# Second graph layer of a two-layer GNN and mixture-of-experts kernel: the scaling of the attention output moves from VectorE to ScalarE

## The reference, cut to what matters

```
x = x + L0_gnn(layernorm(x), adj)
x = x + L0_ffn(layernorm(x))            # 8 experts, top 2, 512 hidden
x = x + L1_gnn(layernorm(x), adj)       # this one ends in a relu
x = x + L1_ffn(layernorm(x))            # 8 experts, top 2, 256 hidden

# L1_gnn
Wh = h @ W
e  = leaky_relu(src(Wh)[:, :, None] + dst(Wh)[:, None, :], 0.2)
attention = softmax(where(adj > 0, e, -9e15), axis=2)
return relu(attention @ Wh)
```

## Time and profile before

| | us |
|---|---|
| median of 3 runs | 964.57 (962.50 to 965.32) |
| the profiled execution's own time | 964.91 |
| its span in the profile | 963.1 |
| DVE busy in the span | 745.8 (77%) |
| PE busy | 670.7 (70%) |
| ACT busy | 499.3 (52%) |
| POOL busy | 548.1 (57%) |
| PE's mean granted clock | 0.815 of full speed |

### The profile page before, as it was taken

How to read it: one execution, slowest core, us unless ns; L and a number is a source line. 1 busy time by engine, 2 the same in 40 slices (tenths; PEclk the granted TensorE clock), 3 DMA queues, 4 the chain that set the end, 5 groups by cost and what they waited for, 6 DMA issues and landing times.

```text
span 963.1 us, 24038 instructions
## 1 busy us (share of the span) xinstructions
PE 670.7 (70%) x6281; PEld 558.7 (58%) x6282; DVE 745.8 (77%) x2826; ACT 499.3 (52%) x1129; POOL 548.1 (57%) x544
## 2 busy tenths in 40 slices
PE   3978777650999999999077788788206777887600
PEld 2656555450799999999066667677204665666400
DVE  6788899853699999999369989997535788787628
ACT  2455665320677777777036655666204555555335
POOL 0027677776276666767200565666772777777720
PEclk9977998855899999999658776777657999899755
DMA  8383333342233322336423444322232333333757
GB/s 223 88 181 107 109 94 95 89 105 64 70 89 87 88 84 83 88 83 176 124 85 121 136 135 131 106 89 67 69 116 74 105 104 98 94 107 98 233 219 321
DMA packets 129404, 111.51 MB, mean 116 GB/s; under 512 B 30306, under 2 KB 112681, under 8 KB 129352
## 3 DMA queue, kind: packets, MB, share of 16 engines
q1 hardware_dynamic: 112072, 77.04, 28.6%
q0 software_dynamic: 17280, 33.87, 10.9%
HBM read 60.32 MB, written 52.36 MB: 117 GB/s over the span
## 4 chain that ended last, share of the span: by engine, by line
PE 28%; issue 22%; DVE 22%; POOL 18%; DMA 5%; ACT 3%; SPq 1%; POOLq 1%; DVEq 0%; ACTq 0%
POOL row_buf L454 12%; PE bank L622 10%; PE bank L636 9%; POOL y_buf L462 6%; DVE xin L954 3%; DVE stat L899 3%; DVE x1w L1006 3%; PE bank L517 2%; PE bank L608 2%; DMA y_buf<-g_y,g_dst 1%; DMA yin<-y_buf 1%; PE bank L514 1%; PE bank L534 1%; ACT xn L697 1%; PE bank L498 1%
## 5 line engine op out<-in xcount | busy, mean ns | idle before, releaser
L454 POOL DMA_INDIRECT row_buf<-pay,slot x256 | 256.4, 1001 | 238.3 <-DVE slot L1075 159.1
L462 POOL DMA_INDIRECT y_buf<-g_y,g_dst x284 | 291.5, 1026 | 137.5 <-issue 88.1
L622 PE MATMUL bank<-g_xT,w 128*128 128x256 f16 x1278 | 171.7, 282 | 1.6 <-ACT g_xT L801 1.1
L801 ACT ACTIVATE g_xT<-bank 128x512 f16<-128x512 f16 x142 | 84.8, 597 | 168.6 <-PE bank L608 164.9
L622 PEld LDWEIGHTS bank<-g_xT,w 128*128 x1278 | 120.4, 101 | 21.1 <-issue 2.5
L608 PE MATMUL bank<-ident,g_in 128*128 128x128 f16 x568 | 58.5, 228 | 83.3 <-DMA g_in<-row_buf 70.2
L636 PE MATMUL bank<-w,g_h 128*128 x1260 | 86.4, 222 | 17.9 <-DVE g_y L1223 17.8
L808 ACT ACTIVATE xn<-bank,b_cols 128x256 f32<-128x256 f32 x216 | 86.8, 474 | 21.5 <-PE bank L622 15.1
L636 PEld LDWEIGHTS bank<-w,g_h 128*128 128x128 f16 x1260 | 77.9, 99 | 26.3 <-issue 23.7
L808 ACT ACTIVATE xt<-bank,b_cols 128x256 f32<-128x256 f32 x210 | 84.5, 475 | 16.6 <-PE bank L622 13.1
L608 PEld LDWEIGHTS bank<-ident,g_in 128*128 128x128 f16 x568 | 38.2, 102 | 91.4 <-issue 75.1
(11 more groups left out here) (194 smaller groups left out, 1379.8 us busy)
## 6 DMA issues: line engine op xcount, KB each, us to landing
g_in<-row_buf SPq DMA_DIRECT2D x142, 130.0 KB, 2.2
yin<-y_buf SPq DMA_DIRECT2D x20, 512.0 KB, 5.0
x_buf<-x1w SPq DMA_DIRECT2D x16, 520.0 KB, 5.6
xin<-x_buf SPq DMA_DIRECT2D x10, 520.0 KB, 4.5
y_buf<-g_y,g_dst POOLq DMA_INDIRECT x284
xin<-in_x_dram SPq DMA_DIRECT2D x8, 512.0 KB, 4.0
adj_in<-in_adj_dram SPq DMA_DIRECT2D x16, 256.0 KB, 3.3
row_buf<-pay,slot POOLq DMA_INDIRECT x256
```

Source lines behind the costliest of these rows:

```text
L454: pool.indirect_dma_start(row_buf[L][:, :], bass.IndirectOffsetOnAxis(ap=slot[q][:, k, t:t + 1], axis=0), pay[q][:, t, :], None).then_inc( ...
L462: pool.indirect_dma_start(y_buf[L][:, :], bass.IndirectOffsetOnAxis(ap=g_dst[k][:, t:t + 1], axis=0), g_y[k][:, t, :], None, bounds_check= ...
L622: last = nc.tensor.matmul(dst, w[:, bass.ds(e * (2 * HID[L]) + (wp * HID[L] + c * P), P)], g_xT[q][:, xp, :], start=(m == 0), stop=(m == 2))
L801: nc.scalar.activation(g_xT[q][:, :, :], x_ps[q], ACT.Copy).then_inc(s.gT_sb, 1)
```

## The change

In layer 1 alone, four edits, which belong together. (1) The reciprocals of the sums leave `add_attention` and become `row_scales`, which DVE runs in the middle of `route` of the block before (after the first of the two rounds that find an expert), for block 0 behind the statistics; it begins with a wait for att_ps. (2) ACT waits for rinv_ready rather than att_ps, and then copies the attention in eight pieces of one tile, each with relu and with the row's rinv as its scale. (3) DVE then adds the block in one tensor_tensor of 128x1024, without a factor. (4) PE's wait ahead of the ranks (L578) is for att_sb, ACT's last copy, in place of rinv_ready. Layer 0 keeps its instructions in their order.

```diff
--- before.py
+++ after.py
@@ -575,7 +575,7 @@
                     attention(L, n)
                     keep_busy(IDLE_ATT[L])
                     if L == 0 or not first:
-                        pe.wait_ge(SL[L].x_done if L == 0 else SL[L].rinv_ready, n + 1)
+                        pe.wait_ge(SL[L].x_done if L == 0 else SL[L].att_sb, n + 1)
                     if not first:
                         ranks(L, n - 1)
                     if not last:
@@ -758,9 +758,9 @@
                     if not first:
                         high_parts(L, *block_at(i, d - 1))
                     if L == 1:
-                        act.wait_ge(s.att_ps, n + 1)
-                        for att, t, m in att_parts[L]:
-                            last_copy = nc.scalar.activation(h_new[:, t:t + m, :], att[:, :, 0:D], ACT.Relu)
+                        act.wait_ge(s.rinv_ready, n + 1)
+                        for t in range(TILES):
+                            last_copy = nc.scalar.activation(h_new[:, t, :], att_tile[1][t][:, 0:D], ACT.Relu, scale=rinv[:, t:t + 1])
                         last_copy.then_inc(s.att_sb, 1)
                     if not first:
                         router(L, n - 1)
@@ -989,22 +989,29 @@
                 V.tensor_scalar(keep[:, :], adj_in[q][:, :, :].rearrange("p t j -> p (t j)"), 0.0, BIG,
                                 ALU.not_equal if L == 0 else ALU.is_gt, ALU.mult).then_inc(s.taken, 1)
 
-            def add_attention(L, n, q, turn, beside):
-
-                s = SL[L]
-                dve.wait_ge(s.att_ps if L == 0 else s.att_sb, n + 1)
-                if L == 0:
-                    V.tensor_tensor(xin[q][:, :, X_END:TILE_W], h_sb[:, :, 0:NE], bc(std1[q][:, :]), ALU.mult)
+            def row_scales(L, n):
+
+                dve.wait_ge(SL[L].att_ps, n + 1)
                 for att, t, m in att_parts[L]:
                     last = V.reciprocal(rinv[:, t:t + m], att[:, :, att_w[L] - 1])
-                width = D + NE if L == 0 else D
-                last.then_inc(s.rinv_ready, 1)
-                wait_past(dve, s.stored[q], 16 * turn)
-                dve.wait_ge(s.rinv_ready, n + 1)
-                for t in range(TILES):
-                    att = att_tile[L][t][:, 0:width] if L == 0 else h_new[:, t, :]
-                    last = V.scalar_tensor_tensor(x1w[q][:, t, X_AT:X_AT + width], att, rinv[:, t:t + 1],
-                                                  xin[q][:, t, X_AT:X_AT + width], ALU.mult, ALU.add)
+                last.then_inc(SL[L].rinv_ready, 1)
+
+            def add_attention(L, n, q, turn, beside):
+
+                s = SL[L]
+                if L == 0:
+                    dve.wait_ge(s.att_ps, n + 1)
+                    V.tensor_tensor(xin[q][:, :, X_END:TILE_W], h_sb[:, :, 0:NE], bc(std1[q][:, :]), ALU.mult)
+                    row_scales(0, n)
+                    wait_past(dve, s.stored[q], 16 * turn)
+                    dve.wait_ge(s.rinv_ready, n + 1)
+                    for t in range(TILES):
+                        last = V.scalar_tensor_tensor(x1w[q][:, t, X_AT:TILE_W], att_tile[0][t][:, 0:D + NE], rinv[:, t:t + 1],
+                                                      xin[q][:, t, X_AT:TILE_W], ALU.mult, ALU.add)
+                else:
+                    wait_past(dve, s.stored[q], 16 * turn)
+                    dve.wait_ge(s.att_sb, n + 1)
+                    last = V.tensor_tensor(x1w[q][:, :, X_AT:X_END], h_new[:, :, :], xin[q][:, :, X_AT:X_END], ALU.add)
                 last.then_inc(s.x_done, 1)
                 dve.wait_ge(s.x_done, n + 1)
                 statistics(x1w[q][:, :, X_AT:X_END], rstd2, nmr2, beside, both=rstd_both if L == 0 else None).then_inc(s.st2, 1)
@@ -1037,6 +1044,8 @@
                     yield
                     ch.did(V.tensor_tensor(hot[:, k, :, :], cand[:, :, :], bc(cmax[:, :]), ALU.is_equal))
                     yield
+                    if k == 0 and L == 1 and not (isinstance(n, int) and n == NBLK - 1):
+                        row_scales(L, n + 1)
                     if k == 0:
                         V.tensor_scalar(tok_run[:, :], tok_run[:, :], float(BLK), None, ALU.add)
                         V.tensor_scalar(pay[q][:, :, D + 1], r1[:, :], -1.0, float(NE), ALU.mult, ALU.add)
@@ -1095,6 +1104,8 @@
                                   iter(()) if first else route(L, *block_at(i, d - 1)))
                     if not first:
                         ch.did(low_parts(L, n - 1, (q + 1) % 2))
+                    if first and L == 1:
+                        row_scales(L, 0)
                     placing = iter(()) if first else places(L, n - 1, (q + 1) % 2)
                     if not over:
                         add_attention(L, n, q, turn, placing)
```

More of the change, by code:

```diff
@@ L990, in take_in @@
                                 ALU.not_equal if L == 0 else ALU.is_gt, ALU.mult).then_inc(s.taken, 1)
+            def row_scales(L, n):
+                dve.wait_ge(SL[L].att_ps, n + 1)
+                for att, t, m in att_parts[L]:
+                    last = V.reciprocal(rinv[:, t:t + m], att[:, :, att_w[L] - 1])
+                last.then_inc(SL[L].rinv_ready, 1)
             def add_attention(L, n, q, turn, beside):
                 s = SL[L]
-                dve.wait_ge(s.att_ps if L == 0 else s.att_sb, n + 1)
                 if L == 0:
+                    dve.wait_ge(s.att_ps, n + 1)
                     V.tensor_tensor(xin[q][:, :, X_END:TILE_W], h_sb[:, :, 0:NE], bc(std1[q][:, :]), ALU.mult)
-                for att, t, m in att_parts[L]:
-                    last = V.reciprocal(rinv[:, t:t + m], att[:, :, att_w[L] - 1])
-                width = D + NE if L == 0 else D
-                last.then_inc(s.rinv_ready, 1)
-                wait_past(dve, s.stored[q], 16 * turn)
-                dve.wait_ge(s.rinv_ready, n + 1)
-                for t in range(TILES):
-                    att = att_tile[L][t][:, 0:width] if L == 0 else h_new[:, t, :]
-                    last = V.scalar_tensor_tensor(x1w[q][:, t, X_AT:X_AT + width], att, rinv[:, t:t + 1],
-                                                  xin[q][:, t, X_AT:X_AT + width], ALU.mult, ALU.add)
+                    row_scales(0, n)
[8 more added lines that the diff above has]
+                    last = V.tensor_tensor(x1w[q][:, :, X_AT:X_END], h_new[:, :, :], xin[q][:, :, X_AT:X_END], ALU.add)
                 last.then_inc(s.x_done, 1)
```

## The result

The changed kernel takes 969.35 us (median of 5, 965.62 to 973.55) against 962.50 for the kernel before beside it (median of 5, 960.74 to 965.32): 1.0067 of it, 95% interval 1.0039 to 1.0095. The forecast was 969.6, 5.0 us above the median of before, with a range of 965.3 to 974.2.

The account below looks back on a forecast made before the run. DVE was taken to bound layer 1's blocks, the loop through ACT and PE being nearly equal. The terms 1.7 - 0.4 + 3.1 - 0.5 + 1.1 = +5.0 us put the median at 969.6, range 965.3 to 974.2.

Parts of the forecast that it names:

- (a): The forecast itself: DVE's reciprocals in route wait for the attention's end in nearly every block; +5.0 us, chance 0.60.
- (1) DVE's work: DVE in each block: reciprocals moved, eight operations become one addition of 1.224 us; 1.1 us less work per block.
- (2) The copies: ACT's eight scaled copies of the attention: 2.44 us, priced from L842, where three copies took 1.15 us.
- (3) and (5): Queues behind the new wait in route: xn starts at K + 3.05, DVE's addition without waiting; both loops close through attention's end.
- K: Start of DVE's reciprocals in the changed kernel, in route; no earlier than 0.05 us after the attention's end.
- (4) PE's wait: PE's wait ahead of the ranks, moved to ACT's last copy at K + 2.8: costs nothing.
- The last block: End of the stage: DVE stands until the attention ends, so its addition and POOL's last two scatters come later; +1.1 us.
- The intervals: Times between attention ends, split by PE's clock: 25.1 us cold, 23.9 warm; block 3 to 4, with DVE's stall, about -0.5.
- warm ones: Two intervals with scores made at 2.4 GHz: 23.9 us after, 24.2 and 24.0 before; together -0.4 us.
- rival (b): DVE stays the bound, with the fast clock for scores, logits and attention; interval 22.1 us, total -3.8 or 960.8, chance 0.09.
- The first interval: Block 0: the copies put xn 2.85 us behind the attention's end, where it was 1.2; +1.7 us.
- cold interval: Interval with scores made at 1.2 GHz: 25.1 us after the change; three of them together +3.1 us, from xn starting later.

Follow-up runs that it names:

- e4: Changed kernel with ACT normalising the next input ahead of the router's exponentials in layer 1's middle steps: 961.01 us, 0.9992 of the kernel before.
- e5: Kernel before with ACT normalising the next input ahead of the router's exponentials in layer 1's middle steps: 963.43 us, 1.0010 of the kernel before.
- e10: Changed kernel with PE signalling the attention bank by bank, reciprocals and copies in three parts, all reciprocals at the change's place: 969.49 us, 1.0044 of before.
- e9: Changed kernel with bank by bank signals, the last part's reciprocals later in route, and ACT normalising before the router's exponentials: 959.98 us, 0.9936 of before.
- e2: Changed kernel with ACT's three unscaled copies and DVE's eight additions put back, keeping the early reciprocals and wait: 972.20 us, 1.0100 of before.
- e12: The changed kernel itself, unaltered, measured again on another chip with a second profile: 969.99 us, 1.0050 of the kernel before.
- e8: Changed kernel with 12 idle matmuls behind layer 1's attention in place of 8: 968.17 us, 1.0051 of the kernel before.
- e3: Kernel before with ACT's copy of the attention in eight pieces without a scale: 964.75 us, 1.0016 of the kernel before.

## Why the prediction was right

The median came out 0.3 us from the forecast, and the interval of the ratio (+3.8 to +9.1 us) holds the forecast's +5.0. The mechanism (a) is shown by the pair e4 and e5 and by e10 to e9, and e2's times agree with it. The size is in part luck, for PE's clock added a loss that the sum did not have. Point by point, with the prediction's own steps:

- (1) DVE's work. The addition takes 1.22 us, as forecast; the tile's instructions, with their shortest, median and longest ns:

```profile
L763 ACT ACTIVATE h_new<-bank,rinv x64: 359/382/412, 502.0 to 677.7; 128x128 f32<-128x128 f32 x64
L1014 DVE TENSOR_TENSOR x1w<-h_new,xin x8: 1215/1220/1227, 504.2 to 679.0; 128x1024 f32<-128x1024 f32 x8
```

- (2) The copies. Eight take 2.18 us, not 2.44. L842 was nearly the right row for one copy (382 ns from PSUM beside some 386), but in a row they overlap more: one starts every 0.25 us instead of every 0.29. The error was free, for ACT's next work waits for hot_any in any case.
- (3) and (5) The queue behind the wait. xn starts 2.98 us behind K (forecast 3.05). DVE waits for the attention in seven blocks, 1 to 2.7 us each; the forecast said six or seven and up to 2.5. Its addition waits for ACT only in block 0. There K is 0.56 us behind the attention, behind the statistics, and xn 2.9 us (forecast 2.85; 2.4 in e12's profile).
- (4) PE's wait. It shows no cost of its own.
- The last block: from the attention's end to the next slots (L1075, here L1084) it was 7.25 us before and is 8.2, so +0.95 for the forecast's +1.1.
- The intervals. Here the sum's terms were off. From one attention's end to the next they are 26.2, 24.5, 24.5, 26.4, 24.5, 26.2 and 22.0 us, 174.3 in all; before, from 504.86 to 672.84, 168.0. That is +6.4 (+6.8 in e12's profile) for the forecast's 1.7 - 0.4 + 3.1 - 0.5 = +3.9. That the stage is only 5.9 longer is an accident ahead of them: from block 0's xn to its attention's end it took 20.3 us instead of 21.8 (e12: 21.7), with the attention at 3.20 us instead of 3.78. The step that failed is "There are two [warm ones]": I kept the clock of each interval as it was before. PE's clock did not stay. ACT waits 5.3 us for scores made at 1.2 GHz and 2.64 for those at 2.4 GHz. Before, three of seven waits are of the short kind; after, the last alone, and in e12 none:

```profile
663.61 0.60 ACT L731 ACTIVATE e_sb<-bank 128x512 f32<-128x512 f32 x1 [2.64 <-PE bank L517]
```

  That interval took 22.0 us, near the 22.1 that rival (b) had worked out for the higher clock throughout. The first interval, which I had at +1.7, became +4.6, with cold scores and with logits of 2.37 us. The two warm ones, which I had at -0.4, became +0.8. Against that, the plain cold interval is 24.5 us, not 25.1, and the three cold ones came to +2.0 for my +3.1. So a part of rival (d) was at work beside (a): in e12's profile its condition, scores at 1.2 GHz in every block, is met in full, and the stage is 7.6 us longer, between the forecast's 5.0 and the 8.6 of (d). Cold scores alone don't make the loss: e4 has them in every block and is level with before.
- The reading of the earlier trace rows in which I gave (d) its low chance was wrong: "after long full work". The windows of the kernel before, ahead of those scores:

```profile
576.00:578.00 2.00, 0.00 (x0) 0.00 (x0) 1.83 (x15) 0.00 (x0) 1.70 (x2) 1.00 0.98 341
578.00:580.00 2.00, 0.00 (x0) 0.00 (x0) 1.90 (x9) 0.76 (x3) 1.39 (x3) 1.00 0.44 156
580.00:582.00 2.00, 1.39 (x20) 1.21 (x20) 1.88 (x10) 2.00 (x6) 1.18 (x1) 0.57 0.12 40
```

  PE stood idle for 4 us at a granted clock of 1.00, and the clock fell after that, as PE worked again. The page "TensorE: Matmul & The Clock Gate" of the Trainium skill (Part 1, on the HAM clock gate), by which the clock follows how busy PE has been recently, agrees with these rows. e8, with a busier PE and the same mean clock, is no evidence against it, since it left the gap ahead of xn's transposes. Whether that gap is what turned the warm scores cold was not tested, and what sets the pattern stays open.
- DVE's 2.66 us without work at its second loop turn, which I carried over into the interval from block 3 to 4, don't appear in the profile after. The forecast -0.5 for that interval came out as -1.0 (27.4 to 26.4).
- Of the signs, the attentions were to end 23.9 to 25.1 us apart; they ended 22.0 to 26.4 apart. The last was to end at 677 and did at 675.5, in an execution whose first ended 3.7 us earlier than before's.

The median matches better than the sum deserves. With executions that spread over 8 us, agreement to 0.3 us is luck. And the forecast added 5.0 to a median of before of 964.57, which came out as 962.50 beside the changed kernel: the medians differ by 6.9 there and by 4.9 on e12's chip. With the stage's +5.9 and +7.6 beside them, the change cost some 5 to 8 us, the forecast's +5.0 is at the low end of that, and what it lacked is the clock.

## What to carry to other kernels

When two loops of nearly equal length share the engines, what is saved in the one that bounds (0.9905 here) can be lost again through a new wait that ties it to the other (1.0067); look for what else stands behind the new wait in each queue (here hot_any, and through ACT's order the next normalisation), and not at the price of the moved operation. Moving a scale to the engine that reads PSUM needs the scale early; signalling the matmuls bank by bank, with the last part's wait moved back in DVE's queue, gave that, and ordering ACT by what the long loop needs first gave the rest. Look at the length of the stage too, when parts ahead of it vary by more than the effect, but not at one profile of it alone.

## What the runs showed of the hardware that was not expected

- DVE's 2.66 us of "issue" ahead of L954, at the second turn of its hardware loop, appear in e5 too (2.34 us), in e2 (2.34) and in e3 (2.64), but not in the changed kernel, nor in any other profile. The four that have them are those in which DVE adds the block in eight operations; the ten without add it in one. Why is not shown.
- The same work of scores makes ACT wait 2.64 us where PE's clock is granted at 1.00 and 5.31 where it is at 0.50. The granted clock from 500 to 680 us was between 0.70 (e12) and 0.79 (e5) in the fourteen profiles; which scores, logits and attentions meet the low clock changed with the kernel's timing, and the intervals of the changed kernel were 22.0 us long with fast scores, 24.5 with slow ones, and 26.2 to 26.4 where logits and attention were slow as well.
- A kernel whose waits all closed through one loop (e4) ran every interval at 23.9 to 24.0 us, with the scores at 1.2 GHz in all of them.
